# Gathering most routed rows of a mixture of experts beside its last expert, and the last expert's rows apart

## What is computed

```python
# layer 0, mixture of experts: E = 8, TOP_K = 2, CAPACITY = 512, H = 1024
probs = jax.nn.softmax(xf @ Wg, axis=-1)
vals, idx = jax.lax.top_k(probs, TOP_K)
w = vals / (jnp.sum(vals, axis=-1, keepdims=True) + 1e-09)
...     # combine[token, e] = w of the choices kept, the first 512 of each expert
for e in range(E):
    ye = jax.nn.gelu(xf @ W1[e] + b1[e]) @ W2[e] + b2[e]
    out = out + combine[:, e][:, None] * ye
x = x + out
# layer 1 then makes q, k and v of x, adds a bias to the scores of 16 heads,
# takes a softmax over 1024 keys and goes on
```

## Time and profile before

| | us |
|---|---|
| median of 3 runs | 2113.58 |
| lowest and highest run | 2109.4, 2113.95 |
| the profiled execution | 2099.86 |
| its span, first to last instruction | 2098.1 |

### The profile page before, as it was taken

How to read it: one execution, slowest core, us unless ns; L and a number is a source line. 1 busy time by engine, 2 the same in 40 slices (tenths; PEclk the granted TensorE clock), 3 DMA queues, 4 the chain that set the end, 5 groups by cost and what they waited for, 6 DMA issues and landing times.

```text
span 2098.1 us, 37599 instructions
## 1 busy us (share of the span) xinstructions
PE 1908.6 (91%) x15665; PEld 1372.2 (65%) x15665; DVE 1121.4 (53%) x2309; ACT 944.6 (45%) x1644; POOL 449.3 (21%) x502
## 2 busy tenths in 40 slices
PE   5888977995988949899999999999999999999998
PEld 3456965773656645667776776766777777777776
DVE  4474443016142126878887888854545543455544
ACT  2212022112242304778887888854454543445522
POOL 1352100004121033212121212112222222233313
PEclk8879567996998979999999999999999999999999
DMA  4000021112242339621100310000000000000001
GB/s 128 0 1 1 1 66 42 57 47 61 81 140 81 101 118 169 128 42 37 33 23 19 104 31 25 19 21 1 1 1 2 1 1 1 27 1 1 2 1 40
DMA packets 85194, 86.94 MB, mean 41 GB/s; under 512 B 34658, under 2 KB 70946, under 8 KB 84898
## 3 DMA queue, kind: packets, MB, share of 16 engines
q1 hardware_dynamic: 79154, 73.81, 13.2%
q0 software_dynamic: 3072, 8.39, 1.4%
q10 hardware_dynamic: 2800, 2.34, 0.4%
HBM read 65.65 MB, written 18.87 MB: 40 GB/s over the span
## 4 chain that ended last, share of the span: by engine, by line
PE 74%; DVE 18%; issue 3%; DMA 2%; POOL 1%; ACT 1%; SPq 0%; DVEq 0%; POOLq 0%
PE PS L1032 7%; DVE arena L1695 7%; PE PS L1024 7%; PE PS L1899 6%; PE PS L1883 6%; PE PS L1838 5%; PE PS L1528 5%; PE PS L1541 5%; PE PS L1873 5%; DVE arena L1700 4%; PE PS L519 3%; PE PS L1520 3%; PE PS L1843 3%; PE PS L1906 1%; PE PS L1933 1%
## 5 line engine op out<-in xcount | busy, mean ns | idle before, releaser
L1695 DVE CUSTOM_DVE_ANT_0 arena<-PS,arena 128x1024 f32<-128x1024 f32 x256 | 312.8, 1222 | 75.3 <-PE PS L1520 62.4
L1528 PE MATMUL PS<-arena 128*128 128x128 f32 x2048 | 281.8, 275 | 20.4 <-DVE arena L1700 20.2
L1619 ACT ACTIVATE arena<-arena 128x1024 f32<-128x1024 f32 x256 | 295.0, 1152 | 9.8 <-DVE arena L1695 9.8
L1528 PEld LDWEIGHTS PS<-arena 128*128 128x128 f32 x2048 | 241.4, 142 | 87.4 <-DVE arena L1700 34.8
L1980 ACT ACTIVATE arena<-arena 128x449 f32<-128x449 f32 (+1 forms) x256 | 162.5, 635 | 190.8 <-DVE arena L2014 190.8
L2069 POOL TENSOR_SCALAR arena<-arena 128x448 f32<-128x448 f32 (+1 forms) x256 | 154.3, 616 | 419.4 <-DVE arena L2005 419.4
L2014 DVE CUSTOM_DVE_ANT_0 arena<-PS,arena 128x448 f32<-128x448 f32 (+1 forms) x256 | 141.2, 590 | 138.9 <-PE PS L1874 138.0
L1615 ACT COPY arena<-PS 128x512 f32<-128x512 f32 x256 | 150.4, 588 | 102.9 <-PE PS L1528 94.7
L1700 DVE COPY arena<-PS 128x512 f32<-128x512 f32 x256 | 175.9, 687 | 1.2 <-PE PS L1528 1.2
L1024 PE MATMUL PS<-arena 128*128 128x512 f32 x384 | 170.2, 601 | 6.6 <-ACT arena L1123 6.6
L1032 PE MATMUL PS<-arena 128*128 128x256 f32 x768 | 172.2, 385 | 0.0
(11 more groups left out here) (279 smaller groups left out, 2657.0 us busy)
## 6 DMA issues: line engine op xcount, KB each, us to landing
arena<-in_L_ffn_W SPq DMA_DIRECT2D x16, 1024.0 KB, 6.6
arena<-prior SPq DMA_DIRECT2D x16, 512.0 KB, 4.0
parts<-arena SPq DMA_DIRECT2D x24, 256.0 KB, 5.4
arena<-parts SPq DMA_DIRECT2D x96, 64.0 KB, 2.9
arena<-parts SPq DMA_DIRECT2D x48, 128.0 KB, 10.5
ye<-arena SPq DMA_DIRECT2D x8, 512.0 KB, 3.5
prior<-arena SPq DMA_DIRECT2D x4, 1024.0 KB, 9.1
arena<-in_xT SPq DMA_DIRECT2D x2, 1024.0 KB, 8.0
```

The source lines that it names most:

```text
L1528: h = e.transpose(PS[:, i, P * j:P * j + P], Sb[z % 3][:, 512 * g + P * j:512 * g + P * j + P], ident)
L1619: e.activation(Sb[z % 3], Sb[z % 3], ACT.Exp, bias=mr[:, z % 4:z % 4 + 1], scale=-1.0).then_inc(s_exp, 1)
L1695: e.tensor_tensor_reduce(Sb[z % 3], ps, Ab[m % 2], 1.0, 3e38, ALU.add, ALU.min, mr[:, z % 4:z % 4 + 1]).then_inc(s_ttr, 1)
```

## The change

- TensorE makes three blocks of expert 7's hidden layer, then expert 6's result, then the other five blocks, then expert 7's result (`EARLY`). The banks are planned in that order. `result` waits for the hidden blocks one by one.
- Expert 7's rows are stored in a table of their own, `yl`. The routing computes from the choices: `GI` and `WE` for experts 0 to 6 (row 0 and weight 0 where the choice is expert 7), `G7` and `W7` for expert 7 (the same where no choice is).
- `ROWS` orders 48 gathers and adds: for batch 0 the 16 of experts 0 to 6, then 8 of expert 7, one a tile; then the same for batch 1. GpSimd starts when experts 0 to 6 are stored, and waits for expert 7's store before the first of `yl`.
- VectorE does the first 16 adds between its evictions of experts 6 and 7, the next 8 behind expert 7, and the 24 of batch 1 in pairs behind all eight projection blocks and the four value steps of batch 0.
- The turns wait by four tiles: T 0 and 1 for tiles 0 to 3, T 2 and 3 for all 8 tiles. In batch 0 the first block of each half of the query projection comes between them. Two waits follow the new order (`store`, `rest`).

```diff
-    Ye = nc.dram_tensor("ye", (E * CAP, D), F32, kind="Internal").ap()
+    Ye = nc.dram_tensor("ye", ((E - 1) * CAP, D), F32, kind="Internal").ap()
+    Yl = nc.dram_tensor("yl", (CAP, D), F32, kind="Internal").ap()
...
+    EARLY = 3
     for q in range(E + 1):
         if q < E:
...
             for f in range(8):
+                if q == E - 1 and f == EARLY:
+                    plan_out("eo", q - 1)
                 ring.plan(("eh", q, f), "act")
...
-        if q:
+        if q and q != E - 1:
             plan_out("eo", q - 1)
+
+    ROWS = [z for b in range(B) for z in [(t, k) for t in range(TB_ * b, TB_ * b + TB_) for k in range(2)] + [(t, None) for t in range(TB_ * b, TB_ * b + TB_)]]
...
-    def combined(w, b):
-        w.wait_ge(s_comb, 2 * TB_ * (b + 1))
+    def combined(w, b, t=TB_):
+
+        w.wait_ge(s_comb, 3 * TB_ * b + 2 * TB_ + t)
...
+                        w.wait_ge(*ring.emptied((tag[0] + "h", q, f)))
                         h = e.matmul(PS[:, i, D * j:D * j + D], src[:, f, P * (t + j):P * (t + j) + P], wt[:, f, :], start=f == 0, stop=f == 7)
...
-                hidden("eh", q, xgT[q % 2], 0, exw[q % 2][0])
+                hidden("eh", q, xgT[q % 2], 0, exw[q % 2][0], range(EARLY if q == E - 1 else 8))
...
-                w.wait_ge(*ring.emptied(("eh", q - 1, 7)))
                 result("eo", q - 1, hb[(q - 1) % 2], exw[(q - 1) % 2][1])
+            if q == E - 1:
+                hidden("eh", q, xgT[q % 2], 0, exw[q % 2][0], range(EARLY, 8))
...
+        own.step(e.tensor_scalar(is7, IV, 1.0, None, ALU.is_equal))
+        own.after(own.n)
+        own.step(e.tensor_tensor(of7, WK, is7, ALU.mult))
+        own.step(e.tensor_tensor(is7, sl, is7, ALU.mult))
+        own.after(own.n)
+        own.step(e.tensor_tensor(W7, of7[:, 0, :], of7[:, 1, :], ALU.add))
+        own.step(e.tensor_tensor(WE, WK, of7, ALU.subtract))
+        own.step(e.tensor_tensor(G7f, is7[:, 0, :], is7[:, 1, :], ALU.add))
+        then(e.tensor_tensor(sl, sl, is7, ALU.subtract))
+        then(e.tensor_scalar(G7f, G7f, -float((E - 1) * CAP), 0.0, ALU.add, ALU.max))
         e.tensor_copy(GI, sl).then_inc(s_gi, 1)
+        e.tensor_copy(G7, G7f).then_inc(s_gi, 1)
...
-        K.combine_dve(e, w)
...
+            if q == E - 1:
+                for m in range(2 * TB_):
+                    add_rows(e, w, m)
+        for m in range(2 * TB_, 3 * TB_):
+            add_rows(e, w, m)
+
+    def add_rows(e, w, m):
+
+        t, k = ROWS[m]
+        w.wait_ge(s_g[m % 8], 16 * (m // 8) + 16)
+        if k != 0:
+            w.wait_ge(s_comb, m if k else m - m % TB_)
+        weight = W7[:, t:t + 1] if k is None else WE[:, k, t:t + 1]
+        e.scalar_tensor_tensor(out=X[:, t, :], in0=gt[m % 8], scalar=weight, in1=X[:, t, :], op0=ALU.mult, op1=ALU.add).then_inc(s_comb, 1)
+
+    def fetch_rows(e, w, m):
+        t, k = ROWS[m]
+        if m >= 8:
+            w.wait_ge(s_comb, m - 7)
+        src, at_ = (Yl, G7[:, t:t + 1]) if k is None else (Ye, GI[:, k, t:t + 1])
+        e.indirect_dma_start(gt[m % 8], None, src[:, :], bass.IndirectOffsetOnAxis(ap=at_.bitcast(U32), axis=0)).then_inc(s_g[m % 8], 16)
...
-        for j in range(2):
-            w.wait_ge(s_ye[j], 16 * E // 2)
-        w.wait_ge(s_gi, 2)
-        for t in range(NT):
-            fetch_rows(e, w, t)
+        w.wait_ge(s_gi, 3)
+        w.wait_ge(*ring.filled(("count", 15)))
+        w.wait_ge(s_ye[0], 16 * E // 2)
+        w.wait_ge(s_ye[1], 16 * (E // 2 - 1))
+        for m, (t, k) in enumerate(ROWS):
+            if k is None:
+                w.wait_ge(s_ye[1], 16 * E // 2)
+            fetch_rows(e, w, m)
...
-        return part(0, (0, 1)) + part(1, (2, 3))
+        def part(b, os, first):
+            turns, rest = [("T", b, j) for j in range(4)], [("P", o, c, n) for o in os for c, n in CN]
+            rest = [z for z in rest if z not in first]
+            return turns[:2] + first + turns[2:] + rest + [("V", b, j) for j in range(4)]
+        return part(0, (0, 1), [("P", 0, 0, 0), ("P", 0, 1, 0)]) + part(1, (2, 3), [])
...
-                K.combined(w, b)
+                K.combined(w, b, 4 * (j // 2) + 4)
...
-                if s[1] == 0 and s[0] != "T" and added:
-                    K.add_rows(e, w, added.pop(0))
+                if s[0] == "V" or (s[0] == "P" and s[1] < 2):
+                    for m in added[:2]:
+                        K.add_rows(e, w, m)
+                    del added[:2]
...
-        added = list(range(TB_, 2 * TB_))
+        added = list(range(3 * TB_, 6 * TB_))
```

More of the change, by code:

```diff
@@ L1018, in turned, with hidden @@
             h.then_inc(ring.sem, 1)
-        def hidden(tag, q, src, s0, wt):
-            for f in range(8):
+        def hidden(tag, q, src, s0, wt, fs=range(8)):
+            for f in fs:
                 i = group((tag, q, f))
@@ L1278, in dve @@
                 differ(FORMS[q])
[L1279 to L1301 removed]
+            if q == E - 1:
[16 more added lines that the diff above has]
+        e.indirect_dma_start(gt[m % 8], None, src[:, :], bass.IndirectOffsetOnAxis(ap=at_.bitcast(U32), axis=0)).then_inc(s_g[m % 8], 16)
+    K.add_rows, K.ROWS = add_rows, ROWS
     def pool(e, w, own):
@@ L1379, in prep_steps @@
     def prep_steps():
-        def part(b, os):
-            return [("T", b, j) for j in range(4)] + [("P", o, c, n) for o in os for c, n in CN] + [("V", b, j) for j in range(4)]
-        return part(0, (0, 1)) + part(1, (2, 3))
+        def part(b, os, first):
[3 more added lines that the diff above has]
+        return part(0, (0, 1), [("P", 0, 0, 0), ("P", 0, 1, 0)]) + part(1, (2, 3), [])
     PREP = prep_steps()
@@ L1429, in store @@
         def store(o, c):
-            w.wait_ge(s_lo, 4 * o + 2 * c + 2)
+            w.wait_ge(s_lo, max(CHUNK[("P", o, c, n)] for n in range(2)) + 1)
             for part, src in ((0, HM[o % 2][:, 0, c]), (1, HM[o % 2][:, 1, c]), (2, LO[o % 2][:, c])):
```

25 lines of the change are left out of this document (5 added, 20 removed).

## The result

The changed kernel is slower. Its median is 2118.31 us (20 runs, 2112.91 to 2126.77) against 2111.25 us (20 runs, 2105.67 to 2114.45) for the kernel before, measured beside it: a ratio of 1.0037, interval 1.0026 to 1.0048. The forecast was 2112.0, "the same".

A forecast was written before the change was run, and what follows sets the result against it. TensorE, 91% busy, was taken as the bound, its largest hole a 27.21 us wait for VectorE's adds. Of 6.3 us lead at the first turns, 1.5 was kept: 2113.58 - 1.5 = 2112; range 2106 to 2118.

The forecast's parts named there:

- Expert 6 moved, sixteen gathers beside expert 7, the evictions behind them: Expert stage: expert 6 ends 8.75 us sooner, sixteenth add ends at 762.6, expert 7's evictions wait for it.
- the two rivals by which these gathers would make the kernel slower: Beside expert 7: stretched gather issue delays the evictions (2121.5 or 2117, chance 0.14); adds hold up gathers (2120, chance 0.03).
- the smaller form of the first: Half the stretch of the sixteen gathers beside expert 7, giving 2117; within the 0.14 for that rival.
- First turns: Next stage's first two turns, after eight last-expert gathers: start at 779.0 instead of 785.3, 6.3 us sooner.
- The third starts near 788.6: TensorE's third projection of batch 0 starts near 788.6, its VectorE step at 791.3; the first projection takes 3.2 us.
- the product waits for the copy: After the first two groups of turns, TensorE's product waits 0.82 us for the copy.
- They start 5.1 us later, so the last starts at 807.4: The 32 gathers after the last expert's store start 5.1 us later; the last moves from 802.3 to 807.4.
- these two paths: To the last add: gathers by pitch end at 811.0, VectorE's steps with adds at 811.9.
- Its add ends about 3.6 us later: The last gather's add ends about 3.6 us after that gather starts, at 811.0.
- Only two turns behind the last add: Batch 1: two turns take 1.8 us instead of 3.4; projections start at 813.5, 1.8 us sooner.
- A pause elsewhere: TensorE's unexplained 3.35 us stop at 898.42 or a shorter one may go (2107, chance 0.14) or another come (2117, 0.05).
- the one with a new pause: Rival in which another unexplained TensorE pause comes, giving 2117; chance 0.05.

The follow-up runs named there:

- before_again: The kernel before, unchanged, run for a second profile: 2107.9 us, ratio 0.9987.
- t4_old: The changed kernel with the old order of batch 0's preparation steps (four turns, then projections), wait by four tiles kept: ratio 1.0001.
- after_again: The changed kernel, unaltered, run once more for a second profile: ratio 1.0042.
- whole: The changed kernel without the wait by four tiles and the new step order; early gathers and the separate table kept: ratio 1.0003.
- extra6: t4_old with six batch 1 gathers moved ahead of the last expert's, and expert 7's evictions behind 14 adds, not 16: ratio 0.9997.
- before_mid: The kernel before with the two first projection blocks put between batch 0's turns, and the two waits that follow: ratio 0.9994.
- spread7: The changed kernel, where tokens without a row of expert 7 read row p (their partition) instead of row 0: ratio 1.0006; repeated, 1.0017.
- serial: The kernel before with all 32 gathers and adds ahead of the first turns, none beside the preparation: ratio 1.0023.
- hold_t4: t4_old with GpSimd waiting for ScalarE's fourth copy before batch 1's 24 gathers: ratio 1.0036.
- extra6_hold: extra6 with the 18 gathers left of batch 1 held until ScalarE's fourth copy: ratio 1.0017.
- t4_spread: t4_old with tokens lacking a row of expert 7 reading row p instead of row 0: ratio 1.0000.
- after: The changed kernel itself, first profile, against the kernel before: 2118.31 us, ratio 1.0037.
- quiet: The changed kernel with SyncE's loads of queries and keys, and later stores behind them, held until the last add: ratio 1.0023.

## Why the prediction was wrong

Step by step, in us after S (prediction's times less 715.42, the profile's less 713.64):

| step | predicted | measured |
|---|---|---|
| expert 6's last eviction | 20.1 | 20.2 |
| first early gather | 24.4 | 24.7 |
| sixteenth add ends | 47.2 | 47.0 |
| first gather of the last expert | 52.2 | 51.4 |
| first turns | 63.6 | 61.7 |
| third projection's step on VectorE | 75.9 | 85.0 |
| last gather | 92.0 | 102.3 |
| last add ends | 95.6 to 96.5 | 112.8 |
| first projection of batch 1 | 98.1 | 114.7 |
| first score step | 123.9 | 141.3 |

*Expert 6 moved, sixteen gathers beside expert 7, the evictions behind them:* right, within 0.8 us. Neither of the two rivals by which these gathers would make the kernel slower happened; that the smaller form of the first gave 2117, near the 2118.31 measured, is chance. The early gathers keep their pitch of 1.25 us, and GpSimd isn't held up by the adds. The view of the gather line in the changed kernel:

```profile
L1323 POOL DMA_INDIRECT arena<-ye,arena x32: 942/949/1205, 738.3 to 804.9; - x32
L1323 POOL DMA_INDIRECT arena<-yl,arena x16: 942/949/1285, 765.1 to 815.9; - x16
```

The median is 949 ns, as in the earlier trace rows. The rule in the Trainium skill, "SBUF — State Buffer", section "Who interferes with whom", by which a VectorE instruction with two SBUF inputs contends with a GpSimd instruction that reads SBUF, would have asked for gathers lengthened by 48 such adds; the trace again disagrees with it for these short ones. Beside a wide instruction with two SBUF inputs (`differ`, here L1187) the changed kernel has the long row gather of the earlier trace rows again (here L1342):

```profile
606.54 2.28 DVE L1187 TENSOR_TENSOR arena<-arena 128x2048 f32<-128x2048 f32 x1
607.04 2.60 POOL L1342 DMA_INDIRECT arena<-rows,arena  x1 [21.27 <-PE PS L1029]
```

*First turns:* right, and 1.9 us better. The lead over `before_again` is 7.9 us (61.7 against 69.6), more than the 6.3 of the forecast.

*"The third starts near 788.6":* this step failed first. From the first turns to the third projection I had 9.6 us (788.6 - 779.0); it took 18.8 (794.13 - 775.29). It has two terms. The eight products of the first two projections took 6.10 us where I had 3.2 + 1.74 = 4.9; the table of windows of the changed kernel (us, PE, PEld, DVE, ACT, POOL busy, PEclk, DMA share, GB/s) gives the lower of TensorE's two levels for part of this stretch, and then again after the wait of 9.15 us:

```profile
775.00:785.00 10.00, 8.92 (x24) 4.88 (x24) 3.68 (x8) 1.86 (x3) 7.78 (x8) 0.61 0.59 121
785.00:795.00 10.00, 0.87 (x1) 0.50 (x2) 2.92 (x5) 2.88 (x5) 4.05 (x5) 0.74 0.25 66
795.00:800.00 5.00, 5.00 (x7) 2.02 (x6) 1.26 (x3) 0.69 (x1) 0.00 (x0) 0.50 0.01 3
```

The other term is the pause of ScalarE, of which the profile before had none and every other profile with gathers issued beside it has one. I had 0.82 us for "the product waits for the copy"; 794.13 - 784.98 = 9.15 were measured. Of the lead of 7.9 us there is 1.0 left when the projections run again (80.5 us after S against 81.5), with 24 products still to do instead of 28.

*"They start 5.1 us later, so the last starts at 807.4":* the term of the sum that was mis-sized. I kept the old stretch of 39.82 us from first to last of the 32 gathers. It is 47.7 in `before_again`, 45.1 in `t4_old` and 50.8 in the changed kernel, since gathers wait for buffers whose adds stand behind VectorE's steps. I had weighed these two paths separately, gathers by pitch and VectorE by steps; with eight buffers they are one path, in which a stop of the steps is a stop of the gathers.

*"Its add ends about 3.6 us later":* mis-sized too, by the landing. At the start the first add begins 4.6 us after its gather (738.34 to 742.93), at the end 10.1 us. The price of 3.6 came from a place without SyncE's stores and loads beside it. In the kernel before VectorE's own steps covered late landings; with the last expert's eight gathers at the very end nothing does.

*Only two turns behind the last add:* right in kind. From the last pair of turns to the first score step it takes 28.4 us, in `before_again` with all four turns 28.9: 0.6 gained where I had 1.8 to the first projection.

Against `before_again` the parts are: + 4.4 first gather, + 3.1 stretch, - 0.1 from last gather to turns, - 0.6 behind the turns: + 6.8 us. The ratio gives 0.0037 x 2111.25 = 7.8. That the two are so near is partly luck: `after_again` is only 3.7 us over `before_again` at Z. Of the 17.5 us (141.34 - 123.88) between forecast and measurement at the first score step, 9.1 are the base, 6.8 the loss and 1.5 the gain that I had forecast. I read one untypical profile and added 13.7 us to reach the median, as if all of them lay outside the stage of the change; the second profile has 9.1 us more inside it. The scale of the medians is free of that: 1.5 us forecast as gained, 7.1 lost.

*A pause elsewhere:* the 3.35 us of the earlier trace rows didn't move away. The changed kernel has one of 3.48 in the same loop, about as long after the first score step (57.5 and 57.6 us):

```profile
912.44 0.51 PE L1570 MATMUL PS<-arena 128*17 128x128 f32 x7 [3.48 <-issue]
```

So the 0.14 that I gave it to go was unfounded.

The outcome of the forecast, a lead at the first turns that doesn't reach the end, was right as far as `whole` and `t4_old` go: no gain, no loss. That the 32 gathers left are the reason isn't shown, since `extra6`, with 26, lost the difference to VectorE's pause. What I left out is that the order of steps then pushes the same gathers later still. No rival named that; the one with a new pause (0.05, 2117) comes near in number, but meant TensorE in the score loop.

## What to carry to other kernels

Before a sum is made on one profile, take a second one of the same kernel: here the two differed by 2.6 us in all and by 9.1 in the very stage that was changed. Gathers through a few buffers and the adds that free them are one path with the steps behind which the adds stand; an order that stops those steps early costs the gathers, and gathers pushed behind the next transfers land late. Before moving a consumer forward, count what still has to be done after the last producer: here 32 gathers before and after, and no version gained.

## What the runs showed of the hardware

ScalarE stands idle for up to 6.5 us before the third or fourth copy of turned rows, or before the split ahead of them (5.61 in `before_mid`), in fourteen of the fifteen profiles in which gathers are issued beside them; the exception is the first one that I read. The profile names "remote" for most, "issue" in `spread7` (6.45) and in `extra6`, where it is shortest (1.50), and TensorE's product in `whole` (2.26). None is there in `serial`, `hold_t4` and `extra6_hold`, where no gather is issued at that moment.

VectorE has the same idle time in five profiles, always, like ScalarE's, before an instruction that reads what TensorE wrote: 10.53 and 7.89 us before expert 7's second eviction in `extra6_hold` and `extra6`, where gathers are issued beside it, 4.57 in `before_mid`, 4.36 in `hold_t4`, 3.62 in `t4_spread`. TensorE shows the like beside the early gathers (1.74 and 1.03 us at 758 to 760, "issue"). The two longest ended 4.9 us after the start of the last gather that GpSimd issued before it stopped. So `hold_t4` and `extra6_hold`, which have no pause on ScalarE, have one on VectorE.

What the mechanism is stays open. The table of DMA queues lists no instruction packet in the stretch of ScalarE's pause in `after` (784.98 to 793.4 us), `before_again` (786 to 794.29) and `quiet` (792 to 800.13), only packets of gathers, which speaks against a late instruction fetch. Nothing here tells a late semaphore from a crowded memory port.

The time from the start of a gather of 128 rows to its add, with VectorE waiting for it, was 3.0 us for the last gather of `serial` (804.30 to 807.28), where SyncE issues nothing, 4.6 us for the first gather of the changed kernel, and 10.1 us for its last, beside SyncE's stores and loads; 7.1 with the loads held back, 6.5 to 7.4 with rows spread instead of row 0 read by most partitions.

A gather issued beside a 128x2048 instruction of VectorE with two SBUF inputs (2.28 us) took 1.9 to 2.6 us in the changed kernel, beside the 128x256 adds of 0.48 us mostly 0.95.
